# A gated delta-rule layer beside two local-attention layers in fp32: two PSUM banks exchanged, the gate arithmetic split, and VectorE's masked products put ahead of the rotary pair

## What is computed

```
q, k, v = [silu(causal_conv4(x @ W) + b) for W in (Wq, Wk, Wv)]    # 16 heads of 64
q, k = rope(q), rope(k);  q, k = q * rsqrt(sum(q*q)), k * rsqrt(sum(k*k))
beta  = sigmoid(x @ bw + bb)
alpha = exp(-exp(A_log) * softplus(x @ gkw + gkb + dt_bias))
for each token t:                                                 # state S: 64 x 64 per head
    o_t = q_t S + D * sum(q_t * k_t) * v_t
    S   = alpha_t * (S - beta_t k_t (k_t S)) + beta_t k_t v_t
o = (x @ Wg) * silu(rmsnorm(o) * onorm_w);   s = o @ Wo
```

## Time and profile before

| | us |
|---|---|
| median of 3 runs | 4372.28 (4367.95 to 4373.02) |
| the profiled execution | 4367.48 |
| its span, first to last instruction | 4365.7 |
| ScalarE, time from the first tap of n = 0 to that of n = 4: a gated tail | 38.20 |
| the same in an ordinary tail | 25.69 |
| a tile loop, from the last tap of n = 5 to the last masked product | 30.63 |

### The profile page before, as it was taken

One profiled execution on the slowest core, in us unless ns is written; L12 is line 12 of the kernel. 1 busy time (PEld: TensorE's weight loads), 2 busy tenths in 40 slices (PEclk: granted clock), 3 DMA queues, 4 the chain that ended last, 5 costly groups with the idle time before them and its releaser, 6 DMA issues.

```text
span 4365.7 us, 88936 instructions
## 1 busy us (share of the span) xinstructions
PE 3951.9 (91%) x31336; PEld 2670.1 (61%) x31336; DVE 2911.1 (67%) x6250; ACT 1871.6 (43%) x3972; POOL 1581.5 (36%) x1422
## 2 busy tenths in 40 slices
PE   5999999999999999578998998989989988989987
PEld 4555555555555555256766766767767766767675
DVE  3666666665656666488786877867867768768751
ACT  2444444443444444245444444444435435445431
POOL 2111111111111111146564655645555555646542
PEclk9999999999999999789898998998988899989976
DMA  2000000000000000211111111111111111111110
GB/s 103 1 16 1 16 1 16 1 16 1 16 1 16 1 16 1 74 30 25 30 21 36 32 20 47 25 38 24 33 38 20 32 39 28 24 36 32 20 39 6
DMA packets 299140, 105.72 MB, mean 24 GB/s; under 512 B 273265, under 2 KB 286833, under 8 KB 297841
## 3 DMA queue, kind: packets, MB, share of 16 engines
q1 hardware_dynamic: 298624, 99.24, 9.7%
HBM read 73.78 MB, written 25.95 MB: 23 GB/s over the span
## 4 chain that ended last, share of the span: by engine, by line
PE 37%; DVE 11%; issue 5%; ACT 4%; POOL 1%; DMA 0%; SPq 0%; DVEq 0%; POOLq 0%; ACTq 0%
PE d_ps L1855 6%; DVE d_acc L1522 4%; PE d_ps L2034 3%; PE d_ps L2049 3%; PE d_ps L1929 3%; PE d_ps L2068 3%; PE d_ps L1891 2%; PE d_ps L1944 2%; PE d_ps L1956 2%; PE d_ps L1833 2%; PE d_ps L1982 1%; PE d_ps L1908 1%; PE d_ps L1900 1%; PE d_ps L1870 1%; ACT d_acc L1292 1%
## 5 line engine op out<-in xcount | busy, mean ns | idle before, releaser
L231 POOL TENSOR_TENSOR f_qk<-f_m 128x512 f32<-128x512 f32 x128 | 162.3, 1273 | 1391.7 <-DVE f_m L416 1391.7
L1522 DVE SCALAR_TENSOR_TENSOR d_acc<-d_ps,d_cw,d_acc 128x511 f32<-128x511 f32 (+2 forms) x576 | 428.5, 744 | 116.3 <-ACT d_acc L1292 100.5
L1855 PE MATMUL d_ps<-d_xnT,d_wqkv 128*128 128x512 f32 x768 | 404.1, 653 | 0.5 <-DVE d_acc L1522 0.5
L316 ACT ACTIVATE f_pr<-f_sm,f_nb,f_qsc 128x256 f32<-128x256 f32 (+1 forms) x512 | 289.2, 566 | 160.8 <-DVE f_nb L453 158.9
L715 PE MATMUL f_ps<-f_m,f_w 128*128 128x512 f32 (+1 forms) x768 | 338.0, 594 | 14.5 <-DVE f_m L497 14.5
L1292 ACT ACTIVATE d_acc<-d_ps,d_cw 128x512 f32<-128x512 f32 x192 | 148.4, 774 | 350.1 <-PE d_ps L1855 349.2
L1159 POOL TENSOR_TENSOR d_qk<-d_m 128x512 f32<-128x512 f32 x128 | 162.1, 1266 | 302.5 <-DVE d_m L1533 297.3
L447 DVE CUSTOM_DVE_ANT_0 f_sm<-f_ps,f_mask 128x256 f32<-128x256 f32 (+1 forms) x512 | 179.8, 387 | 135.1 <-PE f_ps L621 129.5
L1164 POOL TENSOR_TENSOR d_rn<-d_ss,d_mhalf 128x8 f32<-128x8 f32 x128 | 221.0, 1726 | 127.8 <-DVE d_ss L1543 124.3
L715 PEld LDWEIGHTS f_ps<-f_m,f_w 128*128 128x128 f32 (+1 forms) x768 | 134.1, 178 | 214.7 <-issue 210.9
L646 PE MATMUL f_ps<-f_v,f_pT 128*128 128x64 f32 x1792 | 237.1, 273 | 19.3 <-DVE f_pT L461 19.3
(11 more groups left out here) (211 smaller groups left out, 9426.3 us busy)
## 6 DMA issues: line engine op xcount, KB each, us to landing
d_wqkv<-in_dwqkv SPq DMA_DIRECT2D x33, 768.0 KB, 4.6
blocks_scratch<-d_LT SPq DMA_DIRECT2D x128, 64.0 KB, 2.0
d_T<-inverse_scratch SPq DMA_DIRECT2D x128, 64.0 KB, 2.2
f_xin<-in_x SPq DMA_DIRECT2D x9, 512.0 KB, 4.3
d_xnT<-xnT_scratch SPq DMA_DIRECT2D x9, 512.0 KB, 6.5
xnT_scratch<-f_xT SPq DMA_DIRECT2D x8, 512.0 KB, 3.5
gate_scratch<-f_gate SPq DMA_DIRECT2D x8, 512.0 KB, 2.9
d_xnG<-xnT_scratch SPq DMA_DIRECT2D x8, 512.0 KB, 5.3
```

The source lines that it names most:

```text
L316: nc.scalar.activation(pr[:, u % AHEAD, j, k0:], sm[:, u % AHEAD, j, k0:], ACT.Exp, bias=nb[:, u % AHEAD, j:j + 1], scale=qsc[:, 0, w, h:h ...
L1522: V.scalar_tensor_tensor(out=a[:, k:], in0=ps[:, CV_BANK[n], 0:T - k], scalar=cw[:, X, s * CT + t, TAPS - 1 - k:TAPS - k], in1=a[:, k:], o ...
L1855: last = mm(ps[:, CV_BANK[n], :], wqkv[:, X, k, t * P:(t + 1) * P], xnT[:, k, :], start=k == 0, stop=k == KC - 1)
```

## The change

Three things are changed, all in the delta-rule layer, and no instruction is added or removed.

1. `CV_BANK` gives n = 4 bank 2 and n = 5 bank 4. With it n = 4 waits for the taps of n = 2 in place of those of n = 1, the key transposes of chunk 0 wait for the taps of n = 5, and the solve of chunk 0 (`carried`) waits for those of n = 4.
2. In gated tails VectorE's `gates` is cut after its two bias sums. The rest, `gates_mid`, stands behind the substitution, ahead of the taps of n = 2; `gates_end` stands behind the taps of n = 3. TensorE's `gate_sums` goes behind the projection n = 3, and ScalarE's `gates_end` behind the first tap of n = 3 and the silu of n = 2.
3. In the tile loop VectorE's `products` of chunk c stands ahead of the rotary pair of chunk c + 2.

```
--- before.py
+++ after.py
@@ -777,7 +777,7 @@
 CT = GW // P
 NQ = NT * GH
 O_COL = GP * DH
-CV_BANK = (3, 4, 2, 3, 4, 2)
+CV_BANK = (3, 4, 2, 3, 2, 4)
 IN_BANK = (5, 3, 3, 3)
 G_BANK = (7, 5)
 OT_BANK = (7, 6)
@@ -1428,11 +1428,10 @@
                 out_heads(now[0], now[1])
             if conv:
                 first_tap(i, s, 2)
+                first_tap(i, s, 3)
+                silu(i, 2)
             if gated is not None:
                 gates_end(gated)
-            if conv:
-                first_tap(i, s, 3)
-                silu(i, 2)
             if mid:
                 merge32(mid[0])
             if conv:
@@ -1490,8 +1489,9 @@
                             ALU.add).then_inc(zg_rdy, 1)
             dve.wait_ge(zg_rdy, 1 + 2 * nb + 1)
             V.tensor_tensor(zg[:, :, H:], zg[:, :, H:], rows[:, 2:3, :].to_broadcast([P, NT, H]), ALU.add).then_inc(zg_rdy, 1)
+
+        def gates_mid(nb):
             dve.wait_ge(zg_rdy, 1 + 2 * nb + 2)
-
             dve.wait_ge(eb_rdy, 1 + nb + 1)
             V.tensor_scalar(eb[:, :, :], eb[:, :, :], 1.0, None, ALU.add).then_inc(gstep, 1)
             dve.wait_ge(gstep, 1 + nb * 4 + 1)
@@ -1714,6 +1714,7 @@
                 V.tensor_tensor(xv, xv, ps[:, k, :], ALU.add).then_inc(xo_rdy, 1)
 
         gates(0)
+        gates_mid(0)
         gates_end(0)
 
         def tiles(made, now):
@@ -1730,9 +1731,9 @@
                     state(*now, c)
                     outputs(*now, c)
                 if made:
+                    products(*made, c)
                     if c + 2 < NT:
                         intake(*made, c + 2)
-                    products(*made, c)
 
         def tail(conv, sub, mid, now):
 
@@ -1756,14 +1757,16 @@
                 merge16_mid(mid[0])
             if sub:
                 substitute(sub[0])
+            if gated is not None:
+                gates_mid(gated)
             if conv:
                 conv_items(i, s, range(2, 3))
             if mid:
                 merge16_end(mid[0])
+            if conv:
+                conv_items(i, s, range(3, 4))
             if gated is not None:
                 gates_end(gated)
-            if conv:
-                conv_items(i, s, range(3, 4))
             if mid:
                 merge32(mid[0])
             if done(now) is not None:
@@ -1850,7 +1853,7 @@
                 elif i > 0:
                     pe.wait_ge(cv_acc, 1 + val(i, 6, 0))
             else:
-                pe.wait_ge(cv_acc, 1 + val(i, 6, n - 2))
+                pe.wait_ge(cv_acc, 1 + val(i, 6, 3 if n == 4 else n - 2))
             for k in range(KC):
                 last = mm(ps[:, CV_BANK[n], :], wqkv[:, X, k, t * P:(t + 1) * P], xnT[:, k, :], start=k == 0, stop=k == KC - 1)
             last.then_inc(cv_ps, 1)
@@ -1901,7 +1904,7 @@
             last.then_inc(kq_ps, 1)
             pe.wait_ge(kbg_rdy, 1 + 2 * n())
             if c == 0:
-                pe.wait_ge(cv_acc, 1 + val(i, 6, 5))
+                pe.wait_ge(cv_acc, 1 + val(i, 6, 6))
             pe.wait_ge(kgT_rdy, 1 + n(0))
             for k in range(2):
                 for t in range(GP):
@@ -2009,7 +2012,7 @@
                 pe.wait_ge(kl_rdy, 1 + val(i, NT, NT))
                 pe.wait_ge(v_rdy, 1 + val(i, NT, NT))
                 pe.wait_ge(at_rdy, 1 + val(i, 2 * NT, 2 * NT))
-                pe.wait_ge(cv_acc, 1 + val(min(i + 2, B * NG - 1) if isinstance(i, int) else i + 2, 6, 6))
+                pe.wait_ge(cv_acc, 1 + val(min(i + 2, B * NG - 1) if isinstance(i, int) else i + 2, 6, 5))
             pe.wait_ge(os_rdy, 1 + 2 * n(0))
             if c > 0:
                 pe.wait_ge(st_rdy, 1 + val(i, NT - 1, c))
@@ -2123,10 +2126,10 @@
                 conv(*conv_g, 2)
             if mid:
                 merge16_end(mid[0], 1)
+            if conv_g:
+                conv(*conv_g, 3)
             if gated is not None:
                 gate_sums(gated)
-            if conv_g:
-                conv(*conv_g, 3)
             if put is not None:
                 output_T(put)
             if mid:
```

## The result

The changed kernel takes 4390.21 us (median of 20 runs, 4373.18 to 4404.34), the kernel before 4370.83 in runs beside it: ratio 1.0046, 95% interval 1.0036 to 1.0057, so 20 us slower, between 16 and 25. The forecast was 4391. The profiled execution of the changed kernel took 4387.48 us, its span 4385.7, 20.0 more than before.

The account below looks back on a forecast made before the run. It took TensorE and VectorE as full in ordinary tails, VectorE's exponential wait as bounding gated tails, and a rotary ring as ending last in tile loops. Gates -44, products +67, banks -4 gave +19: 4391 us, range 4335 to 4450.

Parts of the forecast that it names:

- Gates, -44 forecast: Gated tails: VectorE's wait for ScalarE's exponential goes; four tails gain 8.7 us each, three 3.1, 44 us less.
- quick tails: Four of seven gated tails, where the clock had come back before: 8.7 us less each.
- three tails of the earlier trace at half clock: Gated tails where TensorE is the chain: they stay at half clock and gain only the vanished wait, 3.06 us each.
- the stated bound: Gated tails: 61 us less if all seven gain as the quick ones; 21 if all as the slow ones.
- One sign: Gated tails: if right, VectorE's taps of n = 1 start within 0.2 us of the first tap.
- The drain: ScalarE table switches: by the skill page, four at 1.38 us delay n = 2's first tap 5.5 us, leaving about 3 of 8.7.
- Masked products, +67 forecast: Tile loops: products ahead of the rotary pair cost 2.35 us in 23 loops, 1.6 in two, 1.9 in five: 67 more.
- the ring: Tile loop, chunks 0 and 1: rotary pair, GpSimd's add, ScalarE's square and next exponential, then L1559; ends last, 3.26 us.
- The recorded sign: Tile loop: L1559's wait grows to about 1.5 us if right; below 1 us, the rotary ring was not the chain's end.
- the free overlap: Tile loop: masked products fill the ring's time; the sum moved the pair with lengths as timed, products 1.2, pair 1.28 us.
- Banks, -4 forecast: Solve of chunk 0: without the taps it waits for ScalarE's L1390, 0.17 us earlier in at most 24 loops, 4 us less.
- Clock, left out of the sum: Tile loops: sum fails if granted clock differs by more than a few hundredths; rival of clock falls, 4456, chance 0.17.

Follow-up runs that it names:

- single-chunk orders: Two kernels: the kernel before with masked products ahead of the rotary pair at chunk 0 only, 4445.82 us, or at chunk 1 only, 4429.25 us.
- the squares late: Changed kernel with ScalarE's squares of the rotated chunk moved behind the next chunk's exponential and copy of u: 4346.58 us, ratio to before 0.9962.
- the rotation held back: Changed kernel, squares late, with GpSimd's rotation also held until VectorE's key scaling ends and query scaling put ahead of it: 4359.71 us, ratio 0.9983.

## Why the prediction came out right

The time (4391 against 4390) is right in its main mechanisms. The parts measured alone, -50, +69 and -1, are each within 6 us of their forecasts, and most of their errors cancel. In the trace luck has a larger share: the gates gave 18 us more than forecast, and 18 that no term held, in the other tails, the first turns and the end, took that back.

- **Gates, -44 forecast.** The quick tails gained the forecast 8.7 us, 38.20 to 29.53 (one 10.1, and one 5.0, where the clock fell anew). Mis-sized was the step that left the three tails of the earlier trace rows at half clock with 3.1 each: without the wait the clock came back in them too, and they gained 8.65, 11.8 and 8.7. The seven sum to 61.6 in the trace of the changed kernel, and to 61.0 with the gates alone; all seven as quick ones, 61, was the stated bound. One sign failed: the taps of n = 1 start 0.35 us behind the first tap in six of the seven tails, and 0.2 was the limit, because of the bias sum beside GpSimd. The table load ends at 2690.44, the exponential starts at 2690.45 (172 of the trace's 175 loads are followed as closely), and the 8.7 came whole. The drain that the Trainium skill (ScalarE: Activation LUTs, What ACT_TABLE_LOAD costs) adds to a load, by which about 3 of the 8.7 were estimated to be left, did not show.
- **Masked products, +67 forecast.** 63.5 in the loops of the changed kernel; alone 55 in the loops and 69 (62 to 76) in the time. VectorE's idle 0.65 at chunk 0 was 0.57, the ring 3.25 for 3.26, the loop 32.94 for 33. The recorded sign failed all the same: L1559's wait was to grow to 1.5 us and stayed at 0.86, and below 1 was to mean that the ring is not the end. The ring was late as forecast, but VectorE came late to L1559 too, by the 1.02 us that the key scaling had grown. The step that failed is the free overlap: moving the pair also moved GpSimd's rotation, from beside the masked products to beside the key scaling. With that second chain, taking the ring away gives back 0.4 of 2.05 us. So the size came from the ring's sum, but the ring alone doesn't hold it up. For the loops at full clock 1.6 was forecast, and the traces give 0.9 to 1.2; for those long at half clock 1.9, and they went from 36.05 to 37.53.
- **Banks, -4 forecast.** Zero. At the earlier trace rows I took the taps as what releases the solve, with L1390 0.17 us ahead; the solve's distance to the end of L1390 stayed the same after the exchange (0.4 to 0.5 us in 22 of 24 loops), so there the copy had been the releaser. The new wait of n = 4, called free, is free wherever L1966 stands ahead of it; in the first two turns, which have no inverses to finish, TensorE idles 3.8 and 6.3 us there (0.24 before), but those two tails take 20.9 and 24.6 us, as before (20.9 and 24.9).
- **Clock, left out of the sum.** About as many of the 22 loops were long at half clock as before (5 for 4, in other groups), and the mean was 0.937 for 0.932. That it nearly cancelled here was not foreseen: the tails of the single-chunk orders took 38 and 29 us more, and with the squares late some 25 came back.

## What to carry to other kernels

Before moving an instruction, list what its consumers will then run beside, not only what waits for it: here the engine that took over the moved work's output slowed a third instruction by 1 us. A stall that two chains of equal length keep up doesn't go when one is cut, so an experiment that removes one chain must be read at the place, in stretches of like clock, and not by the total alone. The largest gain was the simplest: one engine's in-order list stood in front of ready work, waiting for a slow answer, and only that list had to change.

## What the chip showed

VectorE's instructions with both inputs in SBUF and GpSimd's tensor operations hold each other up; whichever comes second ends late. The key scaling took 0.75 us a pair alone, 1.11 and 2.13 beside GpSimd; L1559 0.68, 0.94 and 1.52; the gates' second bias sum 0.22 and 1.87; GpSimd's rotation 1.27, and 1.60 where L1559 had started before it. VectorE's instructions with one input in PSUM were untouched: the rotary products took 683 ns before and 682 after, the first masked product 684 and 686, so they are the work to put beside GpSimd. The Trainium skill (SBUF — State Buffer, Who interferes with whom) says that a VectorE instruction with two SBUF inputs contends with a GpSimd instruction that reads SBUF, that one with at most one does not (outside the 2-port modes), and that the shared ports are an exclusive lock, for which the order of issue decides who blocks. L1559's end 0.54 us behind GpSimd's L1149 agrees.

The clock's falls form patterns that repeat from batch to batch and change with any new order: kernels of the same loop order had a mean granted clock from 0.930 to 0.941, and the ten runs with the rotation held back spread over 62 us. A difference of some 20 us between two orders of this kernel therefore says little on the order itself, unless stretches of like clock show it too.
